# A gated delta rule in chunks on one core: the small products of even and odd heads issued alternately instead of in runs

## What is computed

```python
def step(carry, ins):
    s, mem = carry
    ...                                   # spikes from mem; alpha, beta from them
    s = s * alpha[..., None]
    pred = jnp.einsum('bhk,bhkv->bhv', kt, s)
    s = s + (beta * kt)[..., None] * (vt - pred)[:, :, None, :]
    out = jnp.einsum('bhk,bhkv->bhv', qt, s)
    return ((s, mem), out)
```

## Time and profile before

| | us |
|---|---|
| median of three runs | 1811.53 |
| lowest and highest run | 1807.76 and 1812.5 |
| the profiled execution's own time | 1813.1 |
| its span, first to last instruction | 1811.4 |
| of it, first chunk's `base` to last chunk's `base` on PE (15 rounds) | 826.1 (327.29 to 1153.34) |
| PE busy, share of the span | 1286.0, 71% |
| DVE busy, share of the span | 1150.2, 63% |

### The profile page before, as it was taken

How to read it: one execution, slowest core, us unless ns; L and a number is a source line. 1 busy time by engine, 2 the same in 40 slices (tenths; PEclk the granted TensorE clock), 3 DMA queues, 4 the chain that set the end, 5 groups by cost and what they waited for, 6 DMA issues and landing times. The chain is left out here.

```text
span 1811.4 us, 26022 instructions
## 1 busy us (share of the span) xinstructions
PE 1286.0 (71%) x8836; PEld 1083.3 (60%) x8836; DVE 1150.2 (63%) x3533; ACT 562.7 (31%) x927; POOL 195.2 (11%) x189
## 2 busy tenths in 40 slices
PE   1300003699988889988889988796697797797785
PEld 1100002588877778877778877694385485485484
DVE  4798896886777877778877778712253253253243
ACT  3200001334434344334344334313242342342321
POOL 2000002111011111011111011102020020020000
PEclk8655556689889999999999999855767667667656
DMA  2000000000000000000000000001000000000000
GB/s 68 0 1 1 1 1 1 1 1 0 0 0 0 0 0 0 0 0 0 0 0 0 0 0 1 1 1 55 0 1 1 0 7 0 0 7 1 0 7 6
DMA packets 9466, 7.28 MB, mean 4 GB/s; under 512 B 2872, under 2 KB 7547, under 8 KB 9406
## 3 DMA queue, kind: packets, MB, share of 16 engines
q1 hardware_dynamic: 7886, 5.07, 1.0%
q10 hardware_dynamic: 1520, 1.48, 0.3%
HBM read 5.50 MB, written 1.05 MB: 4 GB/s over the span
## 5 line engine op out<-in xcount | busy, mean ns | idle before, releaser
L775 PEld LDWEIGHTS ps<-delta_kq_up,delta_arena 64*128 64x128 f32 x1024 | 124.1, 264 | 63.9 <-ACT delta_kq L530 37.2
L775 PE MATMUL ps<-delta_kq_up,delta_arena 64*128 64x128 f32 x1024 | 130.9, 368 | 36.1 <-ACT delta_kq L530 36.1
L1113 DVE TENSOR_TENSOR delta_tm<-delta_tm,ps 128x256 f32<-128x256 f32 x96 | 40.5, 421 | 157.4 <-PE ps L815 157.4
L872 PE MATMUL ps<-ones,beta_b 1*128 1x1 f32 x8 | 1.8, 346 | 195.2 <-PEq L339 195.2
L872 PEld LDWEIGHTS ps<-ones,beta_b 1*128 1x128 f32 x8 | 1.8, 322 | 196.0 <-issue 196.0
L616 ACT ACTIVATE delta_xf<-ps 128x256 f32<-128x256 f32 (+1 forms) x128 | 49.0, 383 | 204.5 <-PE ps L802 140.3
L813 PE MATMUL ps<-delta_xf,delta_tt 128*128 128x64 f32 x768 | 106.6, 284 | 0.0
L815 PE MATMUL ps<-delta_tt,delta_xf 128*128 128x64 f32 x768 | 106.6, 284 | 0.0
L802 PEld LDWEIGHTS ps<-delta_tm,drive 128*128 128x128 f32 x768 | 95.6, 200 | 17.1 <-DVE delta_zb L964 9.2
L500 POOL TENSOR_TENSOR delta_km<-delta_beta_k,delta_arena 128x512 f32<-128x512 f32 x16 | 32.6, 2037 | 656.0 <-DVE delta_beta_k L1010 656.0
L802 PE MATMUL ps<-delta_tm,drive 128*128 128x64 f32 x768 | 98.5, 284 | 6.2 <-ACT delta_tm L606 6.2
(11 more groups left out here) (360 smaller groups left out, 3093.4 us busy)
## 6 DMA issues: line engine op xcount, KB each, us to landing
out<-x SPq DMA_DIRECT2D x4, 256.0 KB, 2.4
setup_wmod<-in_L_wmod ACTq DMA_DIRECT2D x2, 384.0 KB, 3.4
post_wff<-in_L_attn_Wff SPq DMA_DIRECT2D x3, 256.0 KB
post_w<-in_L_ffn_w SPq DMA_DIRECT2D x2, 256.0 KB
post_fc_q<-in_L_ffn_fc_q SPq DMA_DIRECT2D x2, 256.0 KB
setup_wspike<-in_L_attn_Wspike ACTq DMA_DIRECT2D x1, 256.0 KB
wq<-in_L_attn_Wq ACTq DMA_DIRECT2D x1, 256.0 KB
wk<-in_L_attn_Wk SPq DMA_DIRECT2D x1, 256.0 KB
```

The costliest lines, as they stand in the source:

```text
L775: ins = eng.matmul(m.ps[:, at + n, P * (h // 2):P * (h // 2) + P], up_lift[s][ks, cs], m.kq_up[s][ks, :, half], start=True, stop=True)
```

## The change

In `base` the groups are now taken in pairs, and within a pair the products alternate between an even and an odd head: heads 0, 1, 2, 3, then 4, 5, 6, 7. The banks are the same as before, and the semaphore steps come in the same order, each behind the last product of its group. The wait for `update`, which stood ahead of group 3, now stands ahead of group 2.

In `blocks` each level runs over the heads 0 to 7 in turn, so that even and odd heads alternate. The banks are the same. `up..a` is stepped behind head 6 and `up..b` behind head 7, where `up..a` used to come after the fourth product. The wait for `base3`, which stood ahead of each half at levels 32 and 64, stands once ahead of the level.

No product is added or taken away, and nothing changes in the programs of DVE, ACT, POOL and SP.

```diff
-                for n in range(4):
-
-                    if n == 3:
+                for n in range(0, 4, 2):
+
+                    if n == 2:
                         eng.wait_ge(vector_back, vec.before("update", i))
-                    for j, h in enumerate(base_heads(n)):
-                        ks, cs = head(h)
-                        ins = eng.matmul(m.ps[:, (n + 1) % 4, 256 * j:256 * j + 256], m.km[ks, cs], m.kq_base[ks, :, cs], start=True, stop=True)
-                    ins.then_inc(tensor_back, pe.one(f"base{n}"))
+                    for j in range(2):
+                        for e in range(2):
+                            ks, cs = head(base_heads(n + e)[j])
+                            ins = eng.matmul(m.ps[:, (n + e + 1) % 4, 256 * j:256 * j + 256], m.km[ks, cs], m.kq_base[ks, :, cs], start=True, stop=True)
+                            if j:
+                                ins.then_inc(tensor_back, pe.one(f"base{n + e}"))
...
-                    for n, x in enumerate(HALVES):
-                        if s >= 32:
-                            eng.wait_ge(vector_back, vec.at("base3", i))
-                        for h in range(n, H, 2):
-                            ks, cs = head(h)
-                            half = slice(HD * (h // 2), HD * (h // 2) + HD)
-                            ins = eng.matmul(m.ps[:, at + n, P * (h // 2):P * (h // 2) + P], up_lift[s][ks, cs], m.kq_up[s][ks, :, half], start=True, stop=True)
-                        ins.then_inc(tensor_back, pe.one(f"up{s}{x}"))
+                    if s >= 32:
+                        eng.wait_ge(vector_back, vec.at("base3", i))
+                    for h in range(H):
+                        ks, cs = head(h)
+                        half = slice(HD * (h // 2), HD * (h // 2) + HD)
+                        ins = eng.matmul(m.ps[:, at + h % 2, P * (h // 2):P * (h // 2) + P], up_lift[s][ks, cs], m.kq_up[s][ks, :, half], start=True, stop=True)
+                        if h >= H - 2:
+                            ins.then_inc(tensor_back, pe.one(f"up{s}{HALVES[h % 2]}"))
```

## The result

| | before | after |
|---|---|---|
| median, us (4 runs each) | 1812.01 | 1790.59 |
| lowest and highest run | 1807.76 and 1815.73 | 1789.11 and 1793.22 |
| ratio, 95% interval | | 0.9884 [0.9859, 0.9909] |
| span of the profiled execution | 1811.4 | 1789.4 |
| of it, the 15 rounds | 826.1 | 805.0 |

The account below looks back on a forecast made before the run. A round was bound by DVE to 729.13 us, PE to the joins' end, then DVE. 13 rounds x 1.25 = 16.3 plus 5.2 gave 21.5 us off 1811.5: 1790 us, range 1784 to 1800.

Parts of the forecast that it names:

- The path: PE savings before `spread` (L766) go into idle time, 0; savings from there to the transposes count, up to 1.42 us.
- The length of the groups: L775 groups, paired by alternation: first 2.1 us against 2.82, second at half clock 3.75 against 5.13 or 4.97.
- rival 2: No effect: the passes in L775 already overlap as far as they can; 1811.5 us, chance 0.06.
- Case (a): Second L775 group, clock returns when it does now: 0.8 us per round; as a rival 1798.5 us, chance 0.18.
- case (b): Second L775 group, clock returns earlier, transposes wait for `tt`: up to 1.42 us, taken as 1.25 in 13 rounds; chance 0.66.
- the cap of 1.42 us: Most a round can gain at the transposes (L785): PE comes 1.42 us after their input `tt` is ready.
- The first two rounds: More at half clock, transposes 3.45 and 4.15 us behind `tt`; gains taken as 2.4 and 2.8, together 5.2 us.
- Rival 3: Slower: PE idles before the transposes, clock falls ahead of the joins; 15.4 us per such round, three give 1836; chance 0.10.
- What I had costed at nothing: `base` alternation, first L775 group (levels 8 and 16), earlier `update` wait and later semaphore steps: each 0.

Follow-up runs that it names:

- the two parts alone: Kernel before with only `base` alternating: 1807.64 us, ratio 1.0001; with only levels 8 and 16 of `blocks` alternating: 1809.87 us, ratio 1.0013.
- everything together: Kernel after with level 64 taken out behind `tt` and products without use added in PE's idle times: 1752.38 us, ratio 0.9682.

## Why the prediction was right, point by point

*The path.* That what PE saves ahead of `spread` is worth nothing held. `spread` still starts 10.68 us behind `base`, the idle time there grew by what the group lost, and the two parts alone measured 1.0001 and 1.0013.

*The length of the groups.* Forecast 2.1 and 3.75 us, measured 2.06 and 3.79. Alternation removed all of the difference between L775 and the pace of L837. One of the numbers against rival 2 was misread: the x12 in the earlier trace rows counts passes in progress, and 9 started in that stretch, not 12. The conclusion stands without it, since there are 14 in progress now. The prediction also asked what follows from the reorder window in the Trainium skill, "TensorE: Matmul & The Clock Gate", Part 3 (The mechanism), if the order did not matter. The rows do not show that: the same 32 passes took 2.82 us in runs and 2.06 alternating. They fit the condition in that passage, that the row group of the weight load must not conflict: in a run the next head lies on the same half of the rows, and in alternation on the other.

*Case (a) or case (b).* I forecast (b) for nearly all rounds at 1.25 us each. The 13 rounds behind the first two gave 14.3 us, 1.10 each, against 16.3 forecast. Both cases occur: in four of the 13, with the low stretch of 6.83 us, the gain is 0.9 (case (a), forecast 0.8), and in the other nine 1.0 to 1.3 (case (b)). The term was a little too large for two reasons. The clock falls as before in a third of the rounds, and the cap of 1.42 us was measured from the end of `tt`, while the transposes start 0.22 or 0.25 us behind it even where PE waits. (The prediction counts ten rounds with the stretch of 6.83 us before; they are eleven.)

*My reason for case (b)* failed. It was that denser products bring the clock back sooner, so that the low stretches get shorter. They did not: in the 14 rounds behind the first the time at half clock is the same 6.83 us in eight, 10.24 in five and 3.41 in one. What brought PE to the transposes in time is that the low time lies elsewhere, partly in the first group, where it ends in idle time. That this happened in nine of 13 rounds was not forecast by any step, so the size of this term owes something to luck. Why the stretches moved was not tested. The wider step, that a clock that stays up gives the cap, was: the kernel with five added products reached 53.15 us a round with the old order. So was the weight of the place: in the kernel with the hunk of `base` alone, one round with two low stretches of 3.41 us took 53.34 us with both groups in runs.

*The first two rounds.* Forecast 5.2 us, and the two traces differ by 3.2 + 3.6 = 6.8. But no run shows that the change earned them. The two kernels that are worth nothing take 111.5 us for these rounds, and the kernel after 111.9 and 111.5. The 118.7 of the kernel before belong to its one traced run, in which the clock was at 0.50 for 34.13 us from before the first `base` on, where it was 27.31 in those two. What repeats is the 14.2 to 14.4 us of the other 13 rounds, in both traces of the kernel after against the three with the second group in runs. The rest of the 21.4 us is a difference between runs of the kernel before, which spread over 1804 to 1814 us in 31 further runs. The later comparison of the same two kernels gave a ratio of 0.9922, some 14 us, with its run of 1814.23 us counted in. That the sum hit 1790 is in part luck: one term was 2 us too large, and another came out without its cause.

*Rival 3* was priced wrongly and is nearer than its 0.10 says. The step that failed is the price of 15.4 us, which counted L802 to L829 alone. The rest of the round runs at half clock as well, nearly to the next `base` (to 959.50 us, with `base` at 962.73), and a long round costs 24 us. It decides the kernel with only levels 32 and 64 alternating (1814 to 1961 us), and by its size it explains one run of the changed kernel in 14.

*What I had costed at nothing.* The alternation of `base` and that of levels 8 and 16 are worth nothing alone, but not in company with levels 32 and 64: without them the change is slower than before, with them faster. The rows suggest how. Where the clock falls during the first group, that group takes 4.40 us in runs and 3.36 alternating, so PE idles 1.38 or 2.41 us ahead of `spread`. Behind the longer idle time the clock falls once more, at 826.52, the second group is slow in part (3.37 us), and PE idles only 0.79 us before the transposes. Behind the shorter one the clock stays up, the second group takes 2.06, and PE idles 0.68 and 1.42. It would follow that idle time at a harmless place guards against idle time at a harmful one. But one round of the kernel with the hunk of `base` alone speaks against the idle time as the cause:

```profile
389.84 4.38 PE L777 MATMUL ps<-delta_kq_up,delta_arena 64*128 64x128 f32 x32 [2.39 <-ACT delta_kq L530]
395.61 1.13 PE L768 MATMUL ps<-drive,delta_block_ones 128*128 128x512 f32 x2 [1.39 <-DVE drive L1052]
396.67 4.38 PE L777 MATMUL ps<-delta_kq_up,delta_arena 64*128 64x128 f32 x32
```
```profile
397.19:400.60 3.41, 3.41 (x28) 3.41 (x27) 3.28 (x14) 1.49 (x6) 0.00 (x0) 0.50 0.00 0
```

Behind an idle time of 1.39 us the clock did fall once more there. That kernel differs from the one with levels 32 and 64 alone in two things, the order in `base` and the order in the second group. Which of the two, or the idle time, keeps the second fall away stays open.

## What to carry to other kernels

Products that fill half the rows of the array should alternate between the halves where they stand in long runs of one half (eight passes in `blocks`), at the price of a first semaphore that comes later. In `base`, with its runs of four passes, nothing was to be had (2.12 and 2.16 us). Only the time between the last thing PE waits for and the first thing that waits for PE is paid back. Before making PE faster, look at what it would wait for next, and at the clock behind that wait: here a second group that was shorter by 2.9 us (4.97 to 2.06) could cost 24 us a round through the clock of the joins, and moving two steps of DVE out of the way of `tt` brought about 10 us more. If PE has idle time in every round, a few products without use in it may hold the clock: they gave 0.9891 with the old order, as much as the order of the real ones, and with everything together 0.9682. They have to stay off the path, or they cost what they give (0.9990 and 1.0013). And a difference between two traces is the change's only where it repeats: here 14 of 21 us did.

## What the runs showed of the hardware

A PE that is busy all the time does not soon get its clock back: it was busy for 51.16 of 51.16 us at 0.50, most of it with products of 64 columns, and the clock returned only 3.2 us before the next `base`. In another kernel it returned after 13.65 us, amid the same joins, so this is no fixed time. The same products stay at 1.00 if they begin at 1.00, as in every ordinary round (18.8 us for the joins). So a kernel with phases of small products can run at two speeds, and a short wait ahead of the phase can choose: here 53 or 77 us a round. I had not expected that one such choice would cost 24 us, and by the size of one untraced run in 14 the changed kernel seems to make it as well, nor that products which compute nothing would be worth 1.1%.
